# Two of ten attention products per batch go to GpSimd in batches 0 to 2, with five reorderings beside it

## What is computed

```
mask: j in {i - 2**k} U {i}
h = layernorm(x) * (1 + ca) + sa
q, k, v = h @ Wq.T + bq, h @ Wk.T + bk, h @ Wv.T + bv      # 16 heads
attn = softmax(where(mask, q k^T, 0) / sqrt(16))
x = x + ga * ((attn @ v) @ Wo.T + bo)
h = layernorm(x) * (1 + cb) + sb
x = x + gb * (fp6_blocks(h) @ fp6_blocks(weight).T + bias)
```

## Time and profile before

| | us |
|---|---|
| median of 3 runs (281.5 to 282.77) | 281.88 |
| the profiled execution | 282.66 |
| its span, first to last instruction | 280.8 |
| PE busy, share of the span | 255.1, 91% |
| DVE busy | 254.6, 91% |
| ACT busy | 209.8, 75% |
| POOL busy | 200.2, 71% |
| DMA engines, mean rate | 192 GB/s |

### The profile page before, as it was taken

How to read it: one execution, slowest core, us unless ns; L and a number is a source line. 1 busy time by engine, 2 the same in 40 slices (tenths; PEclk the granted TensorE clock), 3 DMA queues, 4 the chain that set the end, 5 groups by cost and what they waited for, 6 DMA issues and landing times.

```text
span 280.8 us, 4383 instructions
## 1 busy us (share of the span) xinstructions
PE 255.1 (91%) x1356; PEld 161.7 (58%) x1356; DVE 254.6 (91%) x323; ACT 209.8 (75%) x564; POOL 200.2 (71%) x152
## 2 busy tenths in 40 slices
PE   6999996899999998988999899989998988997885
PEld 1754553258636742664558554774557755895664
DVE  3699799999999999999979996999979999999980
ACT  2377887876787995698969987998776676676753
POOL 6201439794976599989997899889999899935100
PEclk9999999999999999999999999999999899999999
DMA  7752986695784599247943597039822875640006
GB/s 222 189 197 76 321 282 198 215 348 187 217 289 150 164 281 295 74 162 244 341 144 96 195 362 247 16 90 368 261 94 84 265 222 178 218 145 14 0 3 224
DMA packets 54387, 53.90 MB, mean 192 GB/s; under 512 B 4095, under 2 KB 52813, under 8 KB 54365
## 3 DMA queue, kind: packets, MB, share of 16 engines
q1 hardware_dynamic: 54364, 53.63, 59.8%
HBM read 44.89 MB, written 8.72 MB: 191 GB/s over the span
## 4 chain that ended last, share of the span: by engine, by line
DVE 33%; PE 27%; ACT 16%; POOL 12%; issue 8%; DMA 2%; SPq 0%; DVEq 0%; POOLq 0%; ACTq 0%
POOL pv_buf L677 8%; DVE prod L1736 8%; DVE pv_buf L1869 6%; PE ps L1089 6%; PE ps L958 5%; ACT x_norm L1196 4%; DVE prod L1869 4%; DVE prod L1725 3%; PE ps L838 3%; PE ps L901 3%; PE ps L856 2%; DMA pv_buf<-in_L_wmod 2%; POOL x_norm L385 2%; ACT x L1239 2%; ACT ps L1342 1%
## 5 line engine op out<-in xcount | busy, mean ns | idle before, releaser
L677 POOL TENSOR_TENSOR pv_buf<-pv_buf 128x1024 f32<-128x1024 f32 x48 | 113.7, 2369 | 10.4 <-DVE pv_buf L1869 6.4
L1736 DVE TENSOR_TENSOR prod<-ps,kT 128x1024 f32<-128x1024 f32 (+4 forms) x70 | 75.0, 1106 | 0.0
L1869 DVE TENSOR_TENSOR pv_buf<-v_shift,ps 128x1024 f32<-128x1024 f32 x49 | 59.0, 1209 | 0.0
L856 PE MATMUL ps<-wT,h_cen 128*128 128x256 f32 x128 | 29.9, 379 | 0.0
L827 PE MATMUL ps<-hT,wT 128*128 128x512 f32 x64 | 29.6, 595 | 0.3 <-ACT hT L1285 0.2
L838 PE MATMUL ps<-hT,wT 128*128 128x512 f32 x64 | 29.4, 599 | 0.0
L1010 PE MATMUL ps<-wo_g,w_raw 128*128 128x256 f32 x112 | 28.1, 397 | 0.0
L856 PEld LDWEIGHTS ps<-wT,h_cen 128*128 128x128 f32 x128 | 23.9, 190 | 6.4 <-issue 3.8
L958 PE MATMUL ps<-prod,sel_sum 128*32 128x512 f32 x208 | 25.0, 598 | 0.6 <-DVE prod L1725 0.3
L1010 PEld LDWEIGHTS ps<-wo_g,w_raw 128*128 128x128 f32 x112 | 22.3, 199 | 4.0 <-issue 0.3
L658 POOL TENSOR_TENSOR rstd<-var,minus_half 128x4 f32<-128x4 f32 x8 | 8.1, 1015 | 22.2 <-ACT var L1223 21.0
(11 more groups left out here) (218 smaller groups left out, 570.1 us busy)
## 6 DMA issues: line engine op xcount, KB each, us to landing
v_shift<-v_rows SPq DMA_DIRECT2D x56, 512.0 KB, 5.6
x_in<-in_L_attn_x SPq DMA_DIRECT2D x8, 512.0 KB, 3.8
v_rows<-v_base SPq DMA_DIRECT2D x8, 512.0 KB, 2.9
x_res<-in_L_attn_x SPq DMA_DIRECT2D x8, 512.0 KB, 6.1
out_x<-outb SPq DMA_DIRECT2D x5, 512.0 KB, 3.8
rows_mod<-mod_rows SPq DMA_DIRECT2D x7, 256.0 KB, 5.3
x<-in_L_wmod SPq DMA_DIRECT2D x1, 1024.0 KB, 8.3
row_ga<-mod_rows SPq DMA_DIRECT2D x8, 128.0 KB, 3.5
```

The lines of the kernel that those rows point to most:

```text
L677: nc.gpsimd.tensor_tensor(dst, dst, ring(b, n)[:, t:NT, :], ALU.add).then_inc(s_add, 1)
L856: mm = nc.tensor.matmul(ps23[:, k2, col:col + D], h_cen[:, k, P * t:P * t + P], wT[:, 2, k, :], start=(t % 2 == 0 and k == 0), stop=(t % 2 ...
L1736: nc.vector.tensor_tensor(prod[:, n, :, o:L], ps01[:, :, o:L], kT[:, b % 2, :, 0:L - o], ALU.mult).then_inc(s_prod, 1)
L1869: nc.vector.tensor_tensor(dst[:, at, :].rearrange("p t (h e) -> p t h e", e=DH), v_n.rearrange("p t (h e) -> p t h e", e=DH), weights, ALU ...
```

## The change

1. **Far products on POOL.** For b < `EARLY` = 3, DVE writes the divided weights of n = 8, 9 first, into a free part of `score_buf` in SBUF (`w_far`, 128 of the 640 per token row; POOL can't read PSUM), and the other 512 by a second instruction. POOL makes both products before its add 1; DVE doesn't. New waits: POOL on the far weights, on V and on the attention transposes of batch b-1; PE, `evacuate_v(b+2)` and the copy of the second half of the next scores on the far products.
2. **Attention by halves.** `attention_transposes` does all parts of channels 0 to 127, releases ACT, then channels 128 to 255. ACT's wait for `x_res` moves behind the evacuations.
3. **Keys ahead of the FFN's transposes.** On PE both halves of `k_rows(b+2)` precede `xd_transposes(b-3)`, which stood between them; ACT's evacuations follow the same order.
4. **Batch 3's codes.** `scale_to_psum` and `dequantise(3)` leave DVE; POOL does `dequantise_early(3)` between adds 6 and 7 of batch 5.
5. **ACT before batch 6.** `norm_after(4)` moves behind `quantised(3)` and `exps(6)`.

```diff
+            def far_product(b, n):
+                t, i = tiles_of(n), FAR.index(n)
+                pool.wait_ge(s_wfar, b + 1)
+                pool.wait_ge(s_v, NC * (b + 1))
+                if b > 0:
+                    pool.wait_ge(s_attp, NC * b)
...
+                                        ALU.mult).then_inc(s_far, 1)
@@ POOL, loop
                     rstd_before(2)
+                if b < EARLY:
+                    far_product(b, 8)
+                    far_product(b, 9)
                 add(b, 1)
...
                 add(b, 6)
+                if not has(b + 3):
+                    dequantise_early(b - 2)
                 add(b, 7)
@@ PE, attention_transposes
-                for i, n in enumerate(FAR[::-1] + [0]):
...
-                        for c in range(NC):
+                if b < EARLY:
+                    pe.wait_ge(s_far, len(FAR) * (b + 1))
+                else:
+                    pe.wait_ge(s_pv, NO * (b + 1))
+                for c in range(NC):
+                    for i, n in enumerate(FAR[::-1] + [0]):
+                        if n == 0:
+                            pe.wait_ge(s_add, NADD * (b + 1))
...
-                mm.then_inc(s_attp, 1)
+                    mm.then_inc(s_attp, 1)
@@ PE, loop
                     k_rows(b + 2, 1)
+                    k_rows(b + 2, 0)
                 if post:
                     xd_transposes(b - 3)
-                if ahead:
-                    k_rows(b + 2, 0)
@@ ACT
                 act.wait_ge(s_sp, 2 * b + 2)
+                if 0 < b <= EARLY:
+                    act.wait_ge(s_far, len(FAR) * b)
                 nc.scalar.activation(s2_sb[:, :], ps23[:, 0, :], ACT.Copy).then_inc(s_s, 1)
...
                     evacuate_k(b + 2, 1)
+                    evacuate_k(b + 2, 0)
                 if has(b - 3):
                     evacuate_xd(b - 3)
-                if ahead:
-                    evacuate_k(b + 2, 0)
...
-                if not norm1:
-                    norm_after(b - 1)
 
             quantised(LAST - 4)
             exps(LAST - 1)
+            norm_after(LAST - 3)
@@ DVE, softmax_weights
-                nc.vector.tensor_tensor(w, w, per_head(z_inv, NS), ALU.mult).then_inc(s_w, 1)
+                if b < EARLY:
+                    first = SLOT[FAR[0]]
+                    nc.vector.tensor_tensor(w_far, w[:, :, first:, :], per_head(z_inv, NS - first),
+                                            ALU.mult).then_inc(s_wfar, 1)
+                    nc.vector.tensor_tensor(w[:, :, 0:first, :], w[:, :, 0:first, :], per_head(z_inv, first),
+                                            ALU.mult).then_inc(s_w, 1)
...
@@ DVE, order
                 pv_product(b, 7)
-                pv_product(b, 8)
-                pv_product(b, 9)
+                if b >= EARLY:
+                    pv_product(b, 8)
+                    pv_product(b, 9)
...
             softmax_max(b)
-            scale_to_psum()
-            dequantise(LAST - 4)
             softmax_weights(b)
```

More of the change, by code:

```diff
@@ L56, in adaln_block @@
     NADD_PRE = 6
+    EARLY = 3
     PE_SUMMED = [7, 8, 9]
@@ L135, in adaln_block @@
         s_sb, s2_sb = score_buf[:, 0:L], score_buf[:, L:2 * L]
+        w_far = score_buf[:, NT * NS * HEADS:NT * (NS + len(FAR)) * HEADS].rearrange("p (t s h) -> p t s h", s=len(FAR),
+                                                                                     h=HEADS)
         d = score_buf[:, 0:NT * NS * HEADS].rearrange("p (t s h) -> p t s h", s=NS, h=HEADS)
@@ L250, in adaln_block @@
         s_add = sem("pv_pool_added")
+        s_wfar = sem("far_weights_ready")
+        s_far = sem("far_product_done")
         s_lacc = sem("pv_last_product_taken")
@@ L892, in attention_transposes @@
                     pe.wait_ge(s_z, b - 1)
-                for i, n in enumerate(FAR[::-1] + [0]):
[L894 to L899, removed]
-                        for c in range(NC):
+                if b < EARLY:
[6 more added lines that the diff above has]
+                            pe.wait_ge(s_add, NADD * (b + 1))
+                        part = product_tiles(b, n)
+                        for t in range(tiles_of(n), NT):
                             mm = nc.tensor.matmul(ps67[:, c, P * t:P * t + P],
@@ L1316, in evacuate_v @@
                     act.wait_ge(s_pv, NO * (b - 1))
+                    if b - 2 < EARLY:
+                        act.wait_ge(s_far, len(FAR) * (b - 1))
                 act.wait_ge(s_vp, NC * b + 2 - k2)
@@ L1339, in evacuate_attention @@
                     evacuate_v(b + 2, 0)
+                act.wait_ge(s_xres, 16 * b + 16)
                 for c in range(NC):
@@ L1357, in evacuate_summed @@
                 act.wait_ge(s_vm, means_of(b) + 1)
-                act.wait_ge(s_attp, b + 1)
+                act.wait_ge(s_attp, NC * (b + 1))
                 act.wait_ge(s_yp, 2 * b)
@@ L1515, in _ @@
                     evacuate_k(b + 2, 1)
+                    evacuate_k(b + 2, 0)
                 if has(b - 3):
                     evacuate_xd(b - 3)
-                if ahead:
-                    evacuate_k(b + 2, 0)
-                if has(b - 3):
                     seed_ffn(b - 3)
@@ L1747, in block_maxima @@
                 dve.wait_ge(s_post, NPOST * n - 2)
-                if 0 < b < TAIL - 1:
+                if 0 < b < TAIL - 1 or b == TAIL:
                     dve.wait_ge(s_xd, b)
@@ L1854, in pv_product @@
                     if b > 0:
-                        dve.wait_ge(s_attp, b)
+                        dve.wait_ge(s_attp, NC * b)
                     dst = far_buf[FAR.index(n)]
@@ L1870, in pv_product @@
                                         v_n.rearrange("p t (h e) -> p t h e", e=DH), weights,
-                                        ALU.mult).then_inc(s_pv, 1)
+                                        ALU.mult).then_inc(s_pv, 1 + len(FAR) if b < EARLY and n == FAR[0] - 1 else 1)
             setup_ffn_weight()
```

18 lines of the change are left out of this document (9 added, 9 removed).

## The result

| | before | after |
|---|---|---|
| median (8 runs each, same chip) | 282.22 us (281.5 to 283.81) | 280.3 us (280.08 to 281.37) |
| ratio | | 0.9932, 95% interval 0.9913 to 0.9952 |
| profiled execution, its span | 282.66, 280.8 us | 280.1, 278.3 us |
| DVE busy | 254.6 us | 249.4 us |
| POOL busy | 200.2 us | 209.4 us |

The change gains 1.9 us in the medians and 2.5 us in the profiled span. The forecast was 2.6, and 279.3 us in absolute terms. It stood on a median of 281.88 of three runs of before, which is 282.22 over eight.

A forecast was written before the change was run, and what follows sets the result against it. POOL's queue up to batch 4's h2 was taken as the bound: start -1.3, far pair +3.1, codes +1.9, waits removed -6.8, waits remaining +0.4, together -2.7, taken as -2.6: 279.3 us against the median 281.88. Range 277.9 to 281.9 us.

The forecast's parts named there:

- start: POOL's stretch from batch 0's inverse deviation to batch 4's h2 begins earlier: -1.3 us.
- far pair: POOL's two far products of batch 2, priced from add and gate rows: +3.1 us, lower end 2.4, upper 4.7.
- codes: Batch 3's conversion on POOL, before add 7 and h2 of batch 4: +1.9 us.
- waits removed: POOL's waits for ACT between batch 0's inverse deviation and batch 4's h2 go: -6.8 us.
- waits that remain: POOL at `modulate`: three near-ties of 0.1 to 0.2 us, +0.4 us in sum.
- rival 4: POOL's far pair takes only 2.4 us, gaining another 0.7: 278.6 us; chance 0.10.
- rival 1: POOL in batches 1 to 3: ACT's norm keeps coming 0.7 us late; gain 0.9, 281.0 us; chance 0.15.
- Keys first: PE before the FFN transposes: waits for ACT's x1 go in two iterations, 1.3 us each.
- Rival 2: PE behind batch 2's seventh add: one slow-clock stretch, some 1.8 us; gain 0.8, 281.1 us; chance 0.12.
- Rival 3: POOL's far products hold up DVE's SBUF reads, 3.1 us per batch: slower, 283.8 us; chance 0.08.
- Rival 5: DVE's wait for POOL at batch 3's add 2 (1.5 us) reaches PE: no change, 281.9 us; chance 0.05.
- What would show it: Profile signs: PE waiting over 2 us near 118; account wrong if POOL's own waits stay over 2 us in sum.

The follow-up runs named there:

- e1: Against the changed kernel, batch 3's codes go back from POOL to DVE, ACT's new order staying: 278.97 us, ratio 0.9875 to before.
- e6: Against the changed kernel, POOL makes batch 2's far pair twice: 282.98 us, ratio 1.0022 to before.
- e2: Against the changed kernel, attention transposes run in one piece over both channel halves: 279.62 us, ratio 0.9904 to before.
- after: The changed kernel itself, all five parts in, first profiled execution: 280.1 us, span 278.3 us.
- e7: Against the changed kernel, POOL makes the far pairs of batches 0 and 1 twice: 282.95 us, ratio 1.0008 to before.
- c2: Against the changed kernel, codes on DVE, attention transposes in one piece, POOL far products in batches 0 and 1 only: 278.57 us, ratio 0.9852 to before.
- e8: Against the changed kernel, ACT makes batch 4's norm ahead of batch 3's codes and batch 6's exponentials again: 281.13 us, ratio 0.9945 to before.
- c1: Against the changed kernel, batch 3's codes on DVE and attention transposes in one piece together: 278.0 us, ratio 0.9844 to before.
- e5: Against the changed kernel, far products on POOL in batches 0 and 1 only (EARLY = 2): 279.59 us, ratio 0.9906 to before.

## Why the prediction was right, and where its terms were off

**The account held.** POOL's queue to batch 4's h2 is the bound, and DVE spends its lead there (3.70 us, forecast 3 to 4). Work taken from POOL in the stretch shows up at the last softmax nearly whole (`e1`: 1.9 gives 1.7), work added too (`e6`: 2.5 gives 2.2). The softmaxes of batches 4, 5 and 6 came 2.7, 4.0 and 4.0 us earlier (forecast 2.5, 4.3 and 4.2). Undone one by one, the five parts are worth +2.5 (keys), +1.4 (far products, 1.0 of it ahead of softmax 1), +1.0 (ACT's order), -1.7 (codes) and -0.6 us (halves). Their sum of 2.6 is what the whole change gives: 1.6 in the distance and, at the upper clock near 45 us, 1.0 ahead of softmax 1.

**The sum at h2 was 0.7 us too good, and two terms in it erred in opposite directions.** By the rows: start -1.55 (forecast -1.3), far pair +2.5 (+3.1), codes +1.9 (+1.9), waits removed -6.8 (the same), waits that remain +2.3 (+0.4). That makes -1.65 where the timeline has -1.98; the other 0.3 us is in no single row. The forecast was -2.7. The end of the kernel then made it up: DVE started on h2 0.25 us after it was there before and 0.04 after the change, softmax 7 gained 2.25 and the span 2.5. So the agreement of 2.5 with 2.6 is better than that of the terms, and by the medians the gain is 1.9.

1. *The far pair*: 1.50 and 1.06 us, 2.5 together. The nearest row was not the add or the gated weight, float32 in all operands, but `dequantise_early`, a product with a factor repeated from element to element along the row; from it the lower bound of 2.4 had been worked out. Choosing the rows by their type was the mistake, worth 0.6 us. That the work is a product does not make the difference: the first operation of `modulate` is a float32 product whose factor is repeated only from tile to tile, and took 2.37 us for 128x1024 like the add. This was rival 4's term; its time did not come, because of the next one.
2. *Waits that remain*: mis-sized by 1.9 us. The three near-ties at `modulate` were not 0.1 to 0.2 us but 0.60, 0.75 and 0.58, and a wait of add on add of 0.4 us came in. This is rival 1: its mechanism was named with 0.7 us in each of three batches, and it came in those three. But not all of it is the halves: without them 1.2 of the 1.9 us at `modulate` stay (`e2`), since the chain of add 7, transposes, `v_rows`, ACT and norm is longer than POOL's way round even so. The sentence that ACT gets the first half at 119.2 and so "isn't hurt more" was the wrong step: what counts is when `v_rows` starts behind the second half, 0.55 us later by the order alone, the very figure of rival 1.
3. *Start*: the stretch started 1.55 us earlier, 0.25 more than forecast; the gains on the way to it were placed differently. From batch 0's softmax to batch 1's it is 27.38 us before and 26.65 after, a gain of 0.73 us instead of 1.0. In the second execution of the change it is 26.40: a gain of 0.98, as forecast. The difference goes with PE's clock near 45 us. The four executions with it at the lower level there (`after`, `e2`, `e7`, `c2`) have 26.65 to 26.99 us, the seven with far products on POOL and the upper level 26.38 to 26.40. From batch 1's softmax to batch 2's the gain was 0.92 us where 0.3 had been forecast. The first execution of the change in a window:

```profile
45.00:46.00 1.00, 1.00 (x7) 1.00 (x6) 1.00 (x2) 0.53 (x1) 1.00 (x1) 0.50 0.73 156
```

**Keys first** was forecast by the waits it removes, 1.3 us in each of two batches; undoing it cost 2.5 us of distance. It is the largest of the five parts. **Far products**: 1.4 us, all of it from batches 0 and 1; batch 2's pair is worth nothing. The sum had it at +3.1 against a wait of 1.56 us removed, but the prediction did not ask whether it could be left out.

**Codes**: the forecast's +1.9 us was right, and says that part 4 loses. The prediction's own sum showed it: it charged POOL 1.9 us and let DVE end in a wait of over 3 us. **The ACT order** was costed at nothing for the end, by DVE's slack. That was wrong: with the codes needed by POOL at 203.6 it carries 1.0 us (`e8`).

**Rivals.** Rival 1 came in part. Rival 2's slow stretch did not come in the two traces of the change, where PE waited 1.63 and 1.64 us and not 2.5. It came once in `e7` behind 2.39 us and did not come in `e6` behind 2.55, so its price is right and its cause, the wait, is not confirmed. Rival 3 is refuted by the rows: DVE's products keep 1209 ns and POOL's adds 2370 with the far products among them, and undoing part 1 made the kernel slower. The Trainium skill's warning (Perfetto Trace Analysis, § Optimizing Scalar/DVE Operations) is wider than what holds here; its GPSIMD Engine Reference, § 1. Specifications, limits the contention to VectorE instructions with two SBUF inputs or in a mode with two ports, and the V products have one of their inputs in PSUM. The rows agree with the narrower statement. Rival 5's wait is there (133.48, 1.02 us, forecast 1.5), and PE, which works without a wait from 129.85 us to the scores at 140.98, doesn't feel it.

**What would show it**: the far pair came at 2.5 and PE's wait at 1.63 us instead of over 2, POOL's waits were 0.4 to 0.8 instead of under 0.3, in sum 2.3 us, just over the 2 us that were to prove the account wrong. Taken at its word, that sign calls the account wrong. The experiments (`e1`, `e6`, `c1`) show that the account stands and that this bound was set too tight. Softmax 1 came at 58.77 instead of 58.4 us; softmax 3, the transposes and DVE's wait came as said.

## What to carry to other kernels

When one engine's queue is the bound, cost every part of a change in that engine's time alone: of the five parts here three put work or delay into it. The pair of batch 2 filled a gap and was worth nothing; the codes and the halves cost 2.3 us together. Here DVE, from which the work had been taken, stood in one wait of 3.70 us: that is the sign that it was taken from the wrong engine. Work put into an idle gap of the critical queue counts by what exceeds the gap: a pair of 2.5 us cost 2.2 where there was no gap left (`e6`), and 0.3 where there had been one of 2.4 (the change against `e5`; there it also took 1.5 us from DVE).

Price an operation that the trace lacks by the row with the same pattern of operands, not by the row with the same type. And before a slow stretch of the clock is put down to a wait, look for a run with as long a wait at the same place: `e7` alone would have shown a cause that `e6` contradicts.

## What the runs showed of the hardware

- A POOL product of two float32 operands, one of them repeated sixteen times along the row, took 1.50 us for 128x768 and 1.06 for 128x512, that is 1.7 ns per element of difference; an add of 128x1024 took 2.37, and so did a product whose factor is repeated only from tile to tile.
- PE's clock fell to its lower level at differing places in executions of kernels that are the same up to there: near 45 us in one execution of the change and not in the next, in the tail in `e1` and `e6`. In all thirteen traces PE stands idle for 2.5 us before about 44 us; behind it the granted clock fell to 0.50 in four and stayed at 1.00 in nine. Where it fell on the FFN products of the tail they took 5.2 to 5.3 us instead of 3.6.
- At the seventh add of batch 2, in front of the same light transposes, it fell behind a PE wait of 2.39 us (`e7`) and did not behind one of 2.55 us (`e6`) or of 1.63 us (the change); one execution each. So these runs show no length of wait that decides it.
